# Six transformer layers on one core: each of the four tiles of a sequence gets its own order on every engine

## The reference

```python
def attn_layer(x, Wqkv, qs, ksc, Wo):            # 16 heads of 64, window 32
    q, k, v = split(x @ Wqkv)
    q = l2norm(q) * qs ; k = l2norm(k) * ksc
    q = q*cos*scale + rotate_half(q)*sin*scale   # k the same with 1/scale
    out = local_attention(q, k, v)               # each window sees itself and the window before it
    return out @ Wo
def ffn_layer(x, g, bln, W1, b1, W2, b2):
    xn = (x - mu) / sqrt(var + 1e-05) * g + bln
    a, gate = split(xn @ W1 + b1)
    return (a * gelu(gate)) @ W2 + b2
for i in range(6):
    x = attn_layer(shift_tokens(x), ...) + x
    x = ffn_layer(shift_tokens(x), ...) + x
```

## Time and profile before

| | |
|---|---|
| median of three runs | 3695.51 us |
| the profiled execution: span from first to last instruction | 3699.1 us |
| part A | until about 620 us |
| part B | about 620 to 3,679 us, 48 sequences |
| PE busy, whole span | 3521.4 us (95%) |
| DVE, ACT, POOL busy, whole span | 3039.5, 2586.6, 2309.1 us |
| instructions | 146,879, of them 63,940 matmuls and as many weight loads |

### The profile page before, as it was taken

How to read it: one execution, slowest core, us unless ns; L and a number is a source line. 1 busy time by engine, 2 the same in 40 slices (tenths; PEclk the granted TensorE clock), 3 DMA queues, 4 the chain that set the end, 5 groups by cost and what they waited for, 6 DMA issues and landing times. The chain is left out here.

```text
span 3699.1 us, 146879 instructions
## 1 busy us (share of the span) xinstructions
PE 3521.4 (95%) x63940; PEld 2694.0 (73%) x63940; DVE 3039.5 (82%) x4947; ACT 2586.6 (70%) x4028; POOL 2309.1 (62%) x1364
## 2 busy tenths in 40 slices
PE   6999996999999999999999999999999999999996
PEld 4777774777777777777777777777777777777774
DVE  5767766988889988888888888888898888888883
ACT  3565554677777777777777777777777777777773
POOL 1110104767777777777777767777777777776761
PEclk9999998999999999999999999999999999999998
DMA  2000001212222222222222222222222222222212
GB/s 75 4 4 7 4 7 43 56 48 58 56 58 63 64 56 58 56 56 62 58 56 58 54 56 64 56 58 55 64 63 58 56 57 54 56 56 54 54 49 68
DMA packets 121989, 188.76 MB, mean 51 GB/s; under 512 B 24942, under 2 KB 43142, under 8 KB 120972
## 3 DMA queue, kind: packets, MB, share of 16 engines
q1 hardware_dynamic: 121356, 179.36, 18.7%
HBM read 24.08 MB, written 4.19 MB: 8 GB/s over the span
## 5 line engine op out<-in xcount | busy, mean ns | idle before, releaser
L1325 POOL TENSOR_TENSOR rc<-rc,rs 128x1024 f32<-128x1024 f32 x384 | 912.9, 2377 | 349.2 <-DVE rs L1391 348.5
L1331 POOL TENSOR_TENSOR rc<-rc,rnorm 128x1024 f32<-128x1024 f32 x384 | 723.7, 1906 | 392.9 <-DVE rnorm L162 331.4
L1385 DVE TENSOR_TENSOR rc<-proj,rope_b 128x1024 f32<-128x1024 f32 x384 | 466.7, 1215 | 96.1 <-ACT squares L1177 89.6
L1177 ACT ACTIVATE squares<-proj 128x1024 f32<-128x1024 f32 x384 | 394.0, 1026 | 151.1 <-PE proj L921 137.6
L1013 PEld LDWEIGHTS ring<-pT,vmoved 64*64 64x64 f32 x18432 | 381.2, 135 | 132.8 <-issue 132.8
L1391 DVE TENSOR_TENSOR rs<-proj,rope_b 128x1024 f32<-128x1024 f32 x384 | 466.2, 1214 | 0.0
L958 PEld LDWEIGHTS ring<-ident,rc 128*128 128x128 f32 x3072 | 364.2, 142 | 137.5 <-issue 52.2
L1399 DVE TENSOR_REDUCE sums<-squares 128x16 f32<-128x1024 f32 x384 | 455.3, 1186 | 1.1 <-issue 0.9
L1013 PE MATMUL ring<-pT,vmoved 64*64 64x32 f32 x18432 | 407.7, 220 | 37.9 <-issue 36.4
L958 PE MATMUL ring<-ident,rc 128*128 128x128 f32 x3072 | 426.3, 277 | 11.6 <-POOL rc L1331 6.6
L1013 PE MATMUL ring<-pT,vown 64*64 64x32 f32 x6144 | 381.9, 219 | 13.8 <-issue 13.8
(11 more groups left out here) (176 smaller groups left out, 7886.1 us busy)
## 6 DMA issues: line engine op xcount, KB each, us to landing
vmoved<-vown SPq DMA_DIRECT2D x576, 128.0 KB
vmoved<-vown SPq DMA_DIRECT2D x192, 192.0 KB
vmoved<-vown SPq DMA_DIRECT2D x576, 64.0 KB
wqkv_raw<-in_L_ffn_Wqkv SPq DMA_DIRECT2D x40, 192.0 KB, 2.7
wo<-in_L_ffn_Wo SPq DMA_DIRECT2D x6, 512.0 KB, 4.2
x_attended<-xtok SPq DMA_DIRECT2D x8, 256.0 KB, 2.0
xtok_c<-x_attended SPq DMA_DIRECT2D x8, 256.0 KB, 4.2
out<-xtok_c SPq DMA_DIRECT2D x8, 256.0 KB, 2.4
```

The costliest lines, as they stand in the source:

```text
L1177: nc.scalar.activation(squares[:, c, :], proj[c][:, :], ACT.Square).then_inc(sq_done, 1)
L1325: nc.gpsimd.tensor_tensor(rc[:, k % 2, c, :], rc[:, k % 2, c, :], rs[:, c, :], ALU.add).then_inc(add_done, 1)
L1331: nc.gpsimd.tensor_tensor(dst, dst, rnorm[:, k % 2, c * HEADS:(c + 1) * HEADS].rearrange("p (h o) -> p h o", o=1).broadcast_to([P, HEADS, ...
L1385: nc.vector.tensor_tensor(rc[:, k % 2, c, :].rearrange("p (h d) -> p h d", h=HEADS), proj[c][:, :].rearrange("p (h d) -> p h d", h=HEADS), ...
```

## The change

`ring_order` and all engines' lists are written as one loop over rounds (`ROUNDS`), with a line for each step of each of the four tiles, so that each tile has its own order. The operations and their operands are the same. V0 and V1 of a tile stand side by side ahead of its scores (in tile 4n+2 between the two score halves, and in tile 4n+5 with a projection between them), the two halves of the scores follow each other in three tiles of four, `weigh(k)` is one call, and the semaphores `proj_full`, `sq_done`, `ss_done`, `turned_done`, `add_done` and `unit_done` are two each, for queries and keys, because these may now pass each other. Waits that the old order made needless are written out (`need(act, scr_full, ...)`, `ring_full` waits in `turns_of` and `less_maxima`). PE's list has 4,536 semaphore instructions in place of 3,827.

```diff
-LAST_STEP = NT + 6
+ROUNDS = range(-1, NSEQ + 2)
 def ring_order():
     out = []
-    for g in range(-1, LAST_STEP + 1):
-        mine = [("T3", g - 1), ("V0", g - 1), ("P0", g - 2), ("P1", g - 2), ("V1", g - 1), ("O0", g - 2), ("O1", g - 2),
-                ("T0", g), ("T1", g), ("T2", g)]
+    for n in ROUNDS:
+        mine = [("O0", 4 * n), ("O1", 4 * n), ("T1", 4 * n + 2), ("T0", 4 * n + 2), ("T2", 4 * n + 2),
...
-            for g in STEPS:
...
-                if tile(g - 1):
-                    score(g - 1, 0)
-                    values(g - 1, 0)
-                if tile(g - 2):
-                    transpose_probs(g - 2, 0)
...
-                    score(g - 1, 1)
...
+            for n in ROUNDS:
...
+                transpose_qk(4 * n + 2, 3)
...
+                variance(n - 1)
+                score(4 * n + 2, 0)
+                values(4 * n + 2, 0)
+                values(4 * n + 2, 1)
+                score(4 * n + 2, 1)
+                transpose_probs(4 * n + 1, 0)
+                transpose_probs(4 * n + 1, 1)
...
+                project(0, 4 * n + 4)
+                weigh(4 * n + 1)
+                project(1, 4 * n + 5)
+                transpose_qk(4 * n + 3, 2)
+                transpose_qk(4 * n + 3, 3)
+                turned(0, 4 * n + 4)
+                spread(n - 1)
+                turned(0, 4 * n + 4)
+                output(n, 0)
...
+                project(0, 4 * n + 5)
+                values(4 * n + 3, 0)
+                values(4 * n + 3, 1)
+                score(4 * n + 3, 0)
+                score(4 * n + 3, 1)
+                transpose_qk(4 * n + 4, 1)
+                transpose_probs(4 * n + 2, 0)
+                turned(0, 4 * n + 5)
+                feed_up(n - 1, 3)
...
+                values(4 * n + 4, 0)
+                values(4 * n + 4, 1)
+                score(4 * n + 4, 0)
+                score(4 * n + 4, 1)
+                weigh(4 * n + 3)
...
+                values(4 * n + 5, 1)
+                score(4 * n + 5, 0)
+                score(4 * n + 5, 1)
+                transpose_probs(4 * n + 4, 0)
```

More of the change, by code:

```diff
@@ L950, in transpose_qk @@
             def transpose_qk(k, i):
+                if not tile(k):
+                    return
                 half, c = divmod(i, 2)
-                if half == 0:
-                    pe.wait_ge(unit_done, 2 * k + c + 1)
+                pe.wait_ge(unit_done[c], k + 1)
                 bank = begin(f"T{i}", k)
@@ L967, in score @@
             def score(k, half):
+                if not tile(k):
+                    return
                 j = k % TILES
-                pe.wait_ge(ring_free, RING[f"T{2 * half + 1}", k] + 1)
-                if half == 0:
-                    need(pe, scr_masked, k)
+                if half == 0 and k == 0:
+                    mask_first_scores()
+                pe.wait_ge(ring_free, max(RING[f"T{2 * half}", k], RING[f"T{2 * half + 1}", k]) + 1)
+                need(pe, scr_masked, k)
                 pe.sem_inc(pe_passed, 1)
@@ L986, in transpose_probs @@
             def transpose_probs(k, i):
-                if i == 0:
-                    pe.wait_ge(prob_done, k + 1)
+                if not tile(k):
+                    return
+                pe.wait_ge(prob_done, k + 1)
                 bank = begin(f"P{i}", k)
@@ L994, in transpose_probs, with weigh @@
                 last.then_inc(ring_full, 1)
[L996 to L1002, removed]
+            def weigh(k):
+                if not tile(k):
+                    return
+                begin("O0", k)
+                begin("O1", k)
+                pe.wait_ge(ring_free, max(RING["P0", k], RING["P1", k]) + 1)
+                pe.wait_ge(moved, (k + 1) * 7 * 16)
                 banks = [ring_bank(f"O{i}", k)[:, :].rearrange("p (q k) -> p q k", q=PAIRS) for i in range(2)]
@@ L1005, in weigh @@
                 last = [None, None]
-                for p in range(4 * half, 4 * half + 4):
+                for p in range(PAIRS):
                     for odd in range(2):
@@ L1016, in weigh, with output @@
                                     start=True, stop=True)
[L1017 to L1021, removed]
+                for i in range(2):
+                    last[i].then_inc(ring_full, 1)
+            def output(n, half):
+                if not seq(n):
+                    return
                 pe.wait_ge(wo_in, 16 * (n // BATCH + 1))
                 pe.wait_ge(ring_free, RING["O1", TILES * n + 2 * half + 1] + 1)
-                proj_emptied(0, g + 1)
                 bank = proj_bank(0, 1 - half)
@@ L1185, in values_out @@
             def values_out(k, b):
+                if not tile(k):
+                    return
+                if k > 1:
+                    act.wait_ge(ring_full, RING["O1", k - 2] + 1)
                 if b == 0:
@@ L1311, in make_rope @@
             def make_rope(half, n):
+                if not starts_layer(n):
+                    return
                 tiles = slice(2 * half, 2 * half + 2)
-                need(pool, turned_done, n * 8 - 4 + 4 * half)
+                for c in range(2):
+                    need(pool, turned_done[c], TILES * n - 2 + 2 * half)
                 pool.wait_ge(qks_in, 32 * (n // BATCH + 1))
@@ L1408, in norms_of @@
                 if tile(k):
-                    dve.wait_ge(ss_done, 2 * k + 2)
+                    for c in range(2):
+                        dve.wait_ge(ss_done[c], k + 1)
                     ss = sums[:, 0:2 * HEADS]
```

676 lines of the change are left out of this document (409 added, 267 removed).

## The result

The changed kernel takes 3884.21 us (median of four runs, 3879.54 to 3891.95) against 3697.16 (3693.23 to 3701.81) for the kernel before on the same chip: 1.050 times as long, 95% interval 1.0486 to 1.0521. The forecast was 3725 with a range up to 3780. Slower was right; a loss of 0.8% was forecast and one of 5.0% came.

The account below looks back on a forecast made before the run. PE was taken to bound the kernel. A round was 60.91 - 1.25 + 3.5 + 0.5 = 63.66 us against 63.04, 30 us more in 48 rounds: 3729, less 3.6 to the median, 3725 us, range 3630 to 3780.

Parts of the forecast that it names:

- Fewer entries: Small-tile runs on PE fall from twelve to eight a round; four merges at 0.31 us gain 1.25 us a round.
- The merge of the two splits: Joining tile 4n+4's scores to `weigh`, two different splits of PE's array; worth anything from 0 to 0.31 us.
- double run: Scores of tile 4n+4 joined with `weigh`, 512 PE instructions; second instruction refill nearly always stops, 1.6 us a round.
- Longer stretches: Longer small-tile runs on PE hide less instruction refill; stops of 3.5 us a round against 1.83, a 1.7 us loss.
- Just-in-time waits: PE waiting for other engines, as its list gets shorter; 0.5 us a round, bounds 0 and 2.5.
- the places that the prediction named: `spread` and `output` wait for tile 4n+4's rotation, the first `feed_up` likewise; each holds by some tenths of a us.
- The clock: The windows of part B were read as all at the full granted clock; no loss was priced for it.
- Semaphore instructions: 709 more on PE, 15 a round, passed ahead of the busy array; taken as 0.
- the first: Stops in whole scores and the 512-instruction run don't grow, 1.9 to 2.1 us a round; 3645 us, chance 0.34.
- The second, just-in-time waits: Five places a round on PE miss by half a us, 2.5 us; 3775 us, at most 3821; chance 0.16.
- Its own sign: PE's waits for the rotation, copies out of the ring or probabilities, summing to over 100 us.
- a quiet round of 59.5 to 59.9: Sign the forecast was right: us between starts of `mean` in an undisturbed round of the changed kernel.

Follow-up runs that it names:

- E7: E5 with the score halves of tiles 4n+3, 4n+4 and 4n+5 taken apart again by value products; 3761.73 us against 3717.85.
- E4: The changed kernel with project(1, 4n+6) put between the scores of tile 4n+4 and the weigh of tile 4n+3; 3791.93 us, 1.0269 of before.
- run 91: Not a follow-up kernel: 91 us is what stops cost in the changed kernel's runs of tile 4n+4's scores with `weigh`; that kernel took 3884.21 us.
- E1: The kernel before without one redundant PE wait (sq_done), so 2,560 PE instructions a round, every 256th at a bad place; 3776.98 us, 1.022 of before.
- E2: E1 with 89 semaphore increments on PE once ahead of the rounds, every 256th at a good place; 3625.01 us, 0.9812 of before.
- E10: The changed kernel with one POOL edit: add_halves(0, 4n+4) ahead of scale_probs(4n+2); 3849.26 us, 1.0409 of before.
- E5: The changed kernel with E4's edit, transposes T1 of tile 4n+4 behind feed_up(3), and 2,560 PE instructions a round at good places; 3717.85 us, 1.0056 of before.
- E6: The changed kernel with only transposes T1 of tile 4n+4 moved behind feed_up(3); 3904.86 us, 1.056 of before.
- E9: E5 with one POOL edit: add_halves(0, 4n+4) ahead of scale_probs(4n+2); 3668.44 us, 0.9915 of before.
- E12: E9 with T1 back in its own place and, on POOL, next_lo(n) ahead of add_halves(1, 4n+3); 3612.55 us, 0.9785 of before.
- E3: The changed kernel without repeated PE waits, with 13 increments a round and 62 once: 2,560 PE instructions a round, good places; 3720.29 us, 1.008 of before.
- E8: E3 with 112 increments ahead of the first round instead of 62, every 256th at bad places; 3818.47 us, 1.033 of before.

## Why the prediction was wrong

*Fewer entries, -1.25 us a round: right as far as measured.* E7 gives 0.30 us a merge where 0.31 was taken, for three of the four. The merge of the two splits, bounded by 0 and 0.31, was not measured by itself; E4, which undoes it, is 92 us faster, so it is worth far less than its double run costs.

*Longer stretches, 3.5 us a round of stops: right, and nearly so by kind.* Lone `weigh` 48.7 us in 48 rounds is 1.0 (1.0 taken), the two lone whole scores 29.4 is 0.6 (0.8), the double run 91 is 1.9 (1.6). The reading of the queue as one packet for 256 instructions, and of the double run as a place that always stops, is shown by E1, E2 and E4. By the Trainium skill's "mostly hidden" ("Runtime: NRT & Kernel Launch", "Instruction fetch mechanics") E1 and E2 would have been alike; they differ by 4%.

*Just-in-time waits, 0.5 us a round: the step that failed.* The term came out at some 2 us. In the changed kernel it is what is left of the 3.63 us a round when -1.2 for merges, +1.8 for stops and +1.2 at most for the clock are taken off, 1.8 more than the 0.3 of before. The view of PE's waits shows most of it: outside the small-tile work PE waits 67 us in 46 rounds, 1.5 a round, where before waited 7. T1's wait for POOL is the largest part, 0.96 us from the last score to T1 where 0.15 is free, and E10 gives back 35 us, 0.7 a round. The low parts of the weights are 0.3. The remaining half us or so isn't placed. With the stops gone (E5) such waits show bare: a quiet round of 62.9 us where PE's own list is near 60 (60.91 - 1.25, and 0.31 given back), with 111 us of waits in 46 rounds, 2.4 a round; but E5 also has T1 later, which cost the changed kernel 21 us (E6).

Of the places that the prediction named, what waits for the rotation is in it, small in the changed kernel (4.2 us) and large in E5; T1 and the weights' low parts it did not name. Its bound of 2.5 held the size; its centre rested on the slack of operations of before at their durations of before. What it missed is the mechanism: the same clamp takes 0.38 us in one order and 0.93 in the other, since it now starts more often, and earlier, in an operation of POOL's. DVE's list is 57.5 us a round (2644.11 / 46) where it was 55, and the part that grew stands in the chain to T1 and `feed_up`. E9 and E10 show it.

*The clock: left out altogether.* It was said to be full in part B. The earlier trace rows had 0.97 in its third line, and the six slow rounds of before each had a stretch at half clock. A stop was priced by the mean of before, 1.2 us; but behind some of the long stops the clock stands at half for 3.4 us or more, and the double run made long ones. The time at half clock grew from 20.5 to 129.7 us, and the growth is worth at most half of itself, +1.2 us a round. So this term, put at nothing, is the second that failed. E12 shows what a fall costs where only a wait is shortened, 3 to 4 us. What it costs behind a stop was not measured by itself.

*Semaphore instructions, 0: right for those that stood in the lists, not as a rule.* E3's 13 increments in one place held the next product back by 1.1 us.

*The rivals.* Stops did grow, so the first fell. The second, just-in-time waits, was half of the truth: 3775 to 3821 by itself, and its limit with the clock's 1.2 us a round, 3821 + 57 = 3878, is near what came. Its own sign, rows of such waits of over 100 us, did not appear: all that PE waits outside the small-tile work is 67 us. The terms' unfavourable bounds together would have given 60.91 - 0.95 + 4.5 + 2.5 = 67.0 us a round against 66.67, but without the clock; that this comes so near is partly luck. The forecast treated as alternatives what came together: stops and waits are losses on the same engine, and each makes gaps to which the clock answers.

What would show it, point by point: a quiet round of 59.5 to 59.9 was not seen (the quickest of the changed kernel took 62.9); `issue` in the scores' line grew past 40 only when its added time is counted (33.1 us shown, 43.3 with it); most stops of `weigh` are in the double run (47 of 87); PE's waits for DVE and ACT are under 1 us a round in the view, but those for POOL, which the sentence left out, are not.

## What to carry to other kernels

Count the engine's instructions in a loop's round and look where every 256th falls when PE runs many small matmuls: a change of order, or of a few semaphores, moves these places, and a comparison of two orders measures their luck too (E1 to E2 is 4%). Fix the count to a multiple of 256 and put the places early in quick runs before comparing.

Before a list is made tighter, look at each small operation on VectorE that reads two SBUF operands and ask what GpSimd will be doing when it starts; and read the clock's column of every window, not only its mean.

## What was not expected of the hardware

- Position decides. In seven traces with a drift or a bad place (before, after, E1, E4, E6, E8, E10) there are 1,156 runs of `weigh` that do not stand behind scores. 223 of them stop with a gap over 1 us, and in all 223 the 256th instruction is at 160 or later; 188 of 188 behind scores stop, by 1.6 us on average.
- In before, after and E1 together, 29 of 52 stops of over 1.7 us in small-tile work are followed by a fall of the granted clock to 0.50 during the stop or within 4 us of its end, 19 of 53 of 1.4 to 1.7 us, and 3 of 108 of 1.0 to 1.4. So in these three traces hardly one of the shorter stops is followed by a fall, and of the longer ones nearly half are, each by 3.4 us or more at half clock. How much time that costs was not measured.
- A burst of increments on PE is not free: 13 cost 1.1 us in E3, about 85 ns each.
- Left open: why E8's scores pass place 239 without a stop when the changed kernel's stop with the place there too (1.4 us at 239), and how much of the changed kernel's loss is the clock alone.
